# Centring the feed-forward tokens as two rounded products behind the fourth step's output product, with the square and the copy of the result in two places

## Chip, cores and metric

The kernel runs on one core of a Trainium2 chip. The metric is the device time of one execution, in microseconds (us).

## What is computed

The input is `x` of shape (4, 512, 128). First comes one mixing layer in closed form (a layer norm, an RWKV-style recurrence, a product), then a layer norm, and then six pairs of attention and feed-forward layers. The change lies in the layer norm of the feed-forward layer; cut to what matters:

```
for i in range(6):
    x = attn_layer(shift_tokens(x), ...) + x            # 16 heads of 64, windows of 32 tokens
    x = ffn_layer(shift_tokens(x), ...) + x

def shift_tokens(t):   # the second half of the channels comes from the token before
    a, s = split(t, 2, -1); s = pad(s, one token in front)[:, :-1]; return concatenate([a, s], -1)

def ffn_layer(x, g, bln, W1, b1, W2, b2):
    mu = x.mean(-1); var = ((x - mu) ** 2).mean(-1)
    xn = (x - mu) / sqrt(var + 1e-05) * g + bln
    a, gate = split(xn @ W1 + b1, 2, -1)
    return a * gelu(gate) @ W2 + b2
```

## The kernel before

**Tiles and items.** Channels lie on the 128 partitions, tokens along the free dimension. An item is one batch row (512 tokens) in one layer: 6 x 4 = 24 items. An item has four steps of 128 tokens, `t` = 0 to 3, so there are 96 steps, numbered through; ten more (`TAIL_STEPS`) drain the pipeline. In a step the attention of its tokens is begun (`project(step, ...)`), and work on earlier steps goes on: scores of step - 2, output product (`merge_heads`, L1497) of step - 3, transposes of the normed queries and keys of step - 1 and step - 2 (`turn_qk`, L1372).

**Order of the work.** Each engine has its own loop over the steps, and the order in it is written out by hand: POOL L891 to L952, DVE L1114 to L1149, ACT L1275 to L1312, TensorE (PE) L1594 to L1645. Between the engines there are only semaphores. Each engine executes strictly in its order, so that one wait holds up all that stands behind it. From step 12 to 95, waits that are implied by others are left out (`lean`, L1316).

**Two kinds of product.** Most products are made with `F32R` operands, a value split into a rounded part (`_hi`) and the rest (`_lo`): `project` (L1340 to L1342) is three passes of 512 columns, hi by hi, hi by lo, lo by hi. A plain float32 product, such as the centring, is one instruction in the kernel that the compiler makes into two (the trace counts them as x2).

**The feed-forward layer of item m** runs in the steps of the items behind it. In step t = 3 of item m + 1:
- `shift_tail` (ACT, L1223, copies L1227 and L1228, first thing in the step) writes the shifted tokens `xs2`.
- `centre` (PE, L1501, product L1509), behind the first two projections, multiplies `xs2` by `center` = I - 1/128 into `bank[5]`.
- `take_centred` (ACT, L1230), in front of `square(step, 0)`, squares the bank into `xsq` (L1236) and copies it to `xc` (L1237).
- `variance` (PE, L1511, products L1517), behind `turn_probs`, waits for both and multiplies `xsq` by a column of means into `bank[4]`. `project(step, V1)`, `turn_qk`, `weigh(step - 2, 0)` (L1465) and `turn_qk` stand behind it.
- `take_var` (DVE, L1082) moves four columns to `norm`.

At the start of step t = 0 of item m + 2 `root` (DVE, L1017 to L1025, nine small instructions, one root for the norms of queries and keys and for the variance) runs; `widen_rstd` (PE, L1526) spreads it over the partitions, `scale_xn` (DVE, L1090) multiplies `xc` by it, `bias_xn` (ACT, L1249, L1251) writes `xn_hi` and `xn`, `split_xn` (POOL, L875, L879) writes `xn_lo`, and `expand`, `gelu`, `gate` and `contract` follow. The score of step t = 0 waits for `scale_xn`.

**The other things that the steps below touch.** `rotate(step, c)` (DVE, L979 and L986) reads projection c for q0, q1, k0, k1; `square(step, c)` (ACT, L1188) squares the same bank behind it; `sum_squares` (DVE, L996) sums, POOL's `add` (L864) adds the rotated halves, and `normalise` (POOL, L872) multiplies by the root. `project(step, K1)` waits for `square(step, 1)` (L1336), since it writes the same bank. Steps with item%4 = 3 and t = 3 ("ending", 15, 31, 47, 63, 79) split two weights of the next layer on POOL (`split_weights`, L129 and L131); items with item%4 = 1 split the feed-forward weights at t = 2 and 3 (`split_w_1`, L908, L910), items with item%4 = 2 split two weights at the ends of t = 2 and t = 3.

**The mask of the scores** is written by `mask_cuts` (L1376) in one piece per product or in two or three; the cuts have no arithmetic meaning, each further piece is one more product. In step 6 `more` is 9.

## Time and profile before

| | |
|---|---|
| median of 3 runs | 1683.49 us (1682.31 to 1683.5) |
| the profiled execution | 1678.35 us |
| its span on the core | 1676.6 us |
| busy: PE / DVE / ACT / POOL | 94% / 86% / 66% / 64% |
| PE clock that was granted, mean over the span | 0.979 |

Read the engines' busy shares first, then the 40 slices, then the windows of single steps, and in a step the timeline of each engine with the idle time in front of an instruction and what ended it, in square brackets. PE is matmul, PEld its weight load, DVE VectorE, ACT ScalarE, POOL GpSimd. The ends of matmuls are modelled and overlap with the start of the next; so a matmul's cost is read from the distance between two starts.

### The profile page before, as it was taken

How to read it: one execution, taken by the hardware profiler on the slowest of the kernel's cores; microseconds unless marked ns; L12 is line 12 of the kernel's file. 1: busy time of each engine (PE TensorE's matmuls, PEld its weight loads, DVE VectorE, ACT ScalarE, POOL GpSimd, SP SyncE). 2: the span in 40 equal slices, each digit the busy share in tenths (PEclk: the TensorE clock that was granted, in tenths of full speed). 3: DMA queues.
4: the chain of work that ended last, by engine and by line, in shares of the span. 5: the costliest groups of instructions: out<-in, count | busy, mean ns of one | idle time of the engine just before them, and what ended most of it. 6: DMA issues, size and time to landing. Idle time of an engine off the chain costs nothing.

```text
span 1676.6 us, 77736 instructions
## 1 busy us (share of the span) xinstructions
PE 1568.2 (94%) x33168; PEld 1271.4 (76%) x33168; DVE 1447.6 (86%) x3173; ACT 1114.9 (66%) x2014; POOL 1068.4 (64%) x1040
## 2 busy tenths in 40 slices
PE   4469999999999999999999999999999999999987
PEld 2247888778878878888778788788887878887874
DVE  8969989889889888889989889888889888898862
ACT  4336677667677667677667766766776766776663
POOL 3646767676666666667576577585676575675640
PEclk7679999999999999999999999999999999999999
DMA  2011111211111211111211111211111111111110
GB/s 88 32 51 45 41 38 40 77 35 41 34 50 38 60 44 40 42 51 29 63 38 53 43 37 42 63 38 53 30 51 41 50 51 47 32 44 41 38 47 14
DMA packets 41086, 75.09 MB, mean 45 GB/s; under 512 B 9472, under 2 KB 22568, under 8 KB 40744
## 3 DMA queue, kind: packets, MB, share of 16 engines
q1 hardware_dynamic: 40744, 70.12, 14.4%
q8 instruction: 265, 4.34, 1.1%
q14 instruction: 77, 0.63, 0.1%
HBM read 20.08 MB, written 2.10 MB: 13 GB/s over the span
## 4 chain that ended last, share of the span: by engine, by line
PE 68%; issue 8%; POOL 8%; DVE 6%; ACT 5%; ACTq 0%; POOLq 0%; DVEq 0%
PE bank L1372 8%; PE bank L1340 7%; PE bank L1423 7%; PE bank L1497 7%; PE wide L1465 7%; PE bank L1342 6%; PE bank L1341 6%; PE bank L1482 4%; PE bank L1577 4%; PE bank L1442 3%; POOL qk L864 3%; POOL qk L872 2%; PE bank L1411 2%; PE bank L1549 2%; PE bank L1553 1%
## 5 line engine op out<-in xcount | busy, mean ns | idle before, releaser
L872 POOL TENSOR_TENSOR qk<-qk,rnorm 128x512 f32<-128x512 f32 x384 | 401.2, 1045 | 344.4 <-DVE rnorm L1025 344.4
L864 POOL TENSOR_TENSOR qk<-qk,qk_sin 128x512 f32<-128x512 f32 x384 | 491.8, 1281 | 146.3 <-DVE qk_sin L986 146.3
L1188 ACT ACTIVATE squares<-bank 128x512 f32<-128x512 f32 x384 | 229.5, 598 | 153.5 <-DVE qk_sin L986 153.3
L996 DVE TENSOR_REDUCE norm<-squares 128x8 f32<-128x512 f32 x384 | 258.5, 678 | 30.5 <-ACT squares L1188 28.3
L1340 PE MATMUL bank<-w_hi,xs_hi 128*128 128x512 f32 x576 | 263.5, 457 | 11.8 <-ACT squares L1188 6.6
L979 DVE TENSOR_TENSOR qk<-bank,tables 128x512 f32<-128x512 f32 x384 | 261.7, 682 | 8.8 <-PE bank L1342 8.6
L986 DVE TENSOR_TENSOR qk_sin<-bank,tables 128x512 f32<-128x512 f32 x384 | 261.4, 681 | 0.6 <-POOL qk L864 0.6
L1372 PE MATMUL bank<-ident,qk 128*128 128x128 f32 x1536 | 225.3, 278 | 6.1 <-POOL qk L872 5.3
L1342 PE MATMUL bank<-w_hi,xs_lo 128*128 128x512 f32 x576 | 228.9, 397 | 0.0
L1341 PE MATMUL bank<-w_lo,xs_hi 128*128 128x512 f32 x576 | 227.9, 396 | 0.4 <-issue 0.4
L1372 PEld LDWEIGHTS bank<-ident,qk 128*128 128x128 f32 x1536 | 180.8, 141 | 44.4 <-POOL qk L872 7.0
L1497 PE MATMUL bank<-o_t,w_o_s 128*128 128x128 f32 x1536 | 187.8, 276 | 2.5 <-DVE probs L1039 1.5
L1497 PEld LDWEIGHTS bank<-o_t,w_o_s 128*128 128x128 f32 x1536 | 179.1, 192 | 3.4 <-issue 3.1
L1465 PEld LDWEIGHTS wide<-v,p_t 64*32 64x32 f32 x12288 | 134.2, 105 | 61.5 <-issue 59.1
L1465 PE MATMUL wide<-v,p_t 64*32 64x65 f32 x12288 | 165.5, 225 | 1.8 <-DVE o L1052 1.1
L1031 DVE TENSOR_REDUCE row_max<-bank 128x8 f32<-128x512 f32 x192 | 123.7, 686 | 47.0 <-PE bank L1423 46.4
L1180 ACT COPY v<-bank 128x512 f32<-128x512 f32 x192 | 113.9, 593 | 75.6 <-PE bank L1342 74.8
L1423 PE MATMUL bank<-k_t,q_t 64*32 64x64 f32 x12288 | 150.4, 225 | 14.4 <-issue 14.1
L1219 ACT COPY o_t<-bank 128x512 f32<-128x512 f32 x192 | 112.3, 585 | 71.1 <-PE bank L1482 71.0
L1204 ACT ACTIVATE probs<-probs 128x512 f32<-128x512 f32 x192 | 121.0, 631 | 56.4 <-DVE probs L1039 50.7
L1423 PEld LDWEIGHTS bank<-k_t,q_t 64*32 64x32 f32 x12288 | 142.0, 105 | 21.5 <-issue 18.6
L1340 PEld LDWEIGHTS bank<-w_hi,xs_hi 128*128 128x128 f32 x576 | 109.7, 191 | 41.3 <-ACT squares L1188 14.3
(181 smaller groups left out, 2724.9 us busy)
## 6 DMA issues: line engine op xcount, KB each, us to landing
v<-v SPq DMA_DIRECT2D x96, 390.0 KB, 3.5
v<-v SPq DMA_DIRECT2D x72, 130.0 KB, 3.6
w_raw<-in_L_ffn_Wqkv SPq DMA_DIRECT2D x36, 256.0 KB, 3.2
w_o_s<-in_L_ffn_Wo SPq DMA_DIRECT2D x6, 512.0 KB, 3.9
w_raw<-in_L_ffn_W SPq DMA_DIRECT2D x6, 341.0 KB, 3.4
mix_x_nat<-in_L_attn_x SPq DMA_DIRECT2D x4, 256.0 KB, 3.4
w_raw<-x_res_scratch SPq DMA_DIRECT2D x4, 256.0 KB, 3.4
out<-w_raw SPq DMA_DIRECT2D x4, 256.0 KB, 3.2
```

The source lines that it names most:

```text
L864: pool.tensor_tensor(qk[:, g % 2, c, :], qk[:, g % 2, c, :], qk_sin[:, (QK_CHUNKS * g + c) % SINES, :], ALU.add).then_inc(added[c], 1)
L872: pool.tensor_tensor(view, view, rnorm[:, g % 2, c * HPC:(c + 1) * HPC].unsqueeze(2) .to_broadcast([P, HPC, DH]), ALU.mult).then_inc(norme ...
L979: dve.tensor_tensor(qk[:, g % 2, c, :].rearrange("p (h d) -> p h d", d=DH), src[:].rearrange("p (h d) -> p h d", d=DH), table(kind).unsque ...
L986: dve.tensor_tensor(qk_sin[:, (old + SINES) % SINES, :].rearrange("p (h a d) -> p h a d", a=2, d=DH // 2), src[:].rearrange("p (h a d) -> ...
L996: dve.tensor_reduce(norm2[:, c * HPC:(c + 1) * HPC], squares[:, c % 2, :].rearrange("p (h d) -> p h d", d=DH), AX.X, ALU.add).then_inc(sum ...
L1340: pe.matmul(bank_of(c)[:], l_hi, w_hi[:, n, :], start=True, stop=False)
L1341: pe.matmul(bank_of(c)[:], l_hi, w_lo[:, n, :], start=False, stop=False)
L1342: pe.matmul(bank_of(c)[:], l_lo, w_hi[:, n, :], start=False, stop=True).then_inc(projected[c], 1)
L1372: mm = pe.transpose(bank[2 + c % 2][:, j * P:(j + 1) * P], qk[:, g % 2, c, j * P:(j + 1) * P], ident[:])
L1423: mm = pe.matmul(bank[4 + r][WINDOW * h:WINDOW * (h + 1), col:col + 2 * WINDOW], q_t[row, pair, WINDOW * w:WINDOW * (w + 1)], k_t[row, pai ...
L1465: mm = pe.matmul(wide[WINDOW * h:WINDOW * (h + 1), w, quad * (DH + 1):(quad + 1) * (DH + 1)], p_t[row, r, 2 * s + m, WINDOW * h:WINDOW * ( ...
L1497: mm = pe.matmul(bank[4][:, 0:P], w_o_s[:, layer % 2, p, :], o_t[:, g % 2, p, :], start=(p == 0), stop=(p == PAIRS - 1))
```

## The change

`xs2` is split like the other F32R operands: ACT rounds it to `xs2_hi` (`round_tail`, in the place where `take_centred` was), POOL subtracts to `xs2_lo` (`split_tail`, between `normalise(step - 1, 0)` and the weight splits or `add(step, 0)`). The two share the memory of `xn_hi` and `xn_lo`. `centre` is two passes with the rounded `center_r`, and stands behind `merge_heads` in place of behind the projection of Q0. The square of the bank stands behind `square(step, 2)` on ACT, the copy `xc` is the first instruction of ACT in the next step (t = 0). `variance` waits for the square alone. Some waits of `score` and `merge_heads` are moved. In step 6 `mask_cuts` cuts six masks more (`more` 9 to 15). `center_r` is made once on DVE.

```diff
--- before.py
+++ after.py
@@ -664,7 +664,7 @@
     STEPS = BLOCKS + TAIL_STEPS
     PAD = WINDOW
     NORMS = QK_CHUNKS * HPC
-    N_CONST = 9
+    N_CONST = 10
     SINES = 3
     FIRST_SPLIT = 3 * NBLK
     with ExitStack() as ctx:
...
@@ -700,6 +701,8 @@
         w_1_hi, w_1_lo = sb("w_1_hi", [P, 2 * NHID, P], F32R), sb("w_1_lo", [P, 2 * NHID, P], F32R)
         xn_hi, xn_lo = sb("xn_hi", [P, SEQ], F32R), sb("xn_lo", [P, SEQ], F32R)
         x1, xs2, hidden = sb("x1", [P, 2, SEQ]), sb("xs2", [P, SEQ]), sb("hidden", [P, NHID, SEQ])
+        xs2_hi, xs2_lo = xn_hi, xn_lo
+        center_r = sb("center_r", [P, P], F32R)
         xc = xn = sb("xc_xn", [P, SEQ])
         xsq = gated = sb("xsq_gated", [P, SEQ])
 
...
@@ -876,14 +879,20 @@
                 if not real(m):
                     return
                 pool.wait_ge(xn_copied, 2 * (m + 1))
-                pool.tensor_tensor(xn_lo[:], xn[:], xn_hi[:].bitcast(F32), ALU.subtract).then_inc(xn_ready, 1)
+                pool.tensor_tensor(xn_lo[:], xn[:], xn_hi[:].bitcast(F32), ALU.subtract).then_inc(lo_ready, 1)
+
+            def split_tail(m):
+                if not real(m):
+                    return
+                pool.wait_ge(xs2_ready, 3 * (m + 1))
+                pool.tensor_tensor(xs2_lo[:], xs2[:], xs2_hi[:].bitcast(F32), ALU.subtract).then_inc(lo_ready, 1)
 
             def add_first_residual(m):
                 if not last(m):
                     return
                 b = m % BATCH
                 pool.wait_ge(x_res_loaded, 16 * (b + 1))
-                pool.wait_ge(xs2_ready, 2 * (m + 1))
+                pool.wait_ge(xs2_ready, 3 * (m + 1))
                 pool.tensor_tensor(x1[:, m % 2, :], x1[:, m % 2, :], x_res, ALU.add).then_inc(x1_full, 1)
 
             split_tokens(0, 0)
@@ -922,6 +931,8 @@
                 if opening:
                     split_weights(layer, K1)
                 normalise(step - 1, 0)
+                if t == 3:
+                    split_tail(item - 1)
                 if item % BATCH == 1 and item < ITEMS and t >= 2:
                     split_w_1(layer, t - 2)
                 if ending:
@@ -961,6 +972,7 @@
                 for j in (NHID - 1, 2 * NHID - 1):
                     dve.tensor_scalar(z[:, j, HID[-1]:P], ident[:, HID[-1]:P], 0.0, 0.0, ALU.mult, ALU.add).then_inc(constants_ready, 1)
             dve.memset(v[:, :, 1, :, DH:DH + 1], 1.0).then_inc(constants_ready, 1)
+            dve.tensor_scalar(center_r[:], center[:], 1.0, 0.0, ALU.mult, ALU.add).then_inc(constants_ready, 1)
             dve.wait_ge(constants_ready, N_CONST)
 
             def rotate(g, c):
@@ -1223,17 +1235,27 @@
                 if not real(m):
                     return
                 act.wait_ge(x1_done, NBLK * (m + 1))
-                need(act, centred, m)
+                need(act, lo_ready, 2 * m - 1)
                 act.copy(xs2[0:half, :], x1[0:half, m % 2, :]).then_inc(xs2_ready, 1)
                 act.copy(xs2[half:P, 1:SEQ], x1[half:P, m % 2, 0:SEQ - 1]).then_inc(xs2_ready, 1)
 
+            def round_tail(m):
+                if not real(m):
+                    return
+                act.wait_ge(xs2_ready, 3 * m + 2)
+                need(act, up_ready, NHID * m)
+                act.copy(xs2_hi[:], xs2[:]).then_inc(xs2_ready, 1)
+
+            def square_centred(m):
+                if not real(m):
+                    return
+                act.wait_ge(centred, m + 1)
+                need(act, hidden_ready, NHID * m)
+                act.activation(xsq[:], bank[5][:], ACT.Square).then_inc(cen_taken, 1)
+
             def take_centred(m):
                 if not real(m):
                     return
-                act.wait_ge(centred, m + 1)
-                need(act, hidden_ready, NHID * m)
-                need(act, up_ready, NHID * m)
-                act.activation(xsq[:], bank[5][:], ACT.Square).then_inc(cen_taken, 1)
                 act.copy(xc[:], bank[5][:]).then_inc(cen_taken, 1)
 
             def late_centred():
@@ -1280,6 +1302,8 @@
                     shift_tokens(item + 1, 0)
                 if t == 3:
                     shift_tail(item - 1)
+                if t == 0:
+                    take_centred(item - 2)
                 take_v(step, 0)
                 take_qk(step - 2, 0)
                 if t == 1:
@@ -1288,7 +1312,7 @@
                 if t == 0:
                     bias_xn(item - 2)
                 if t == 3:
-                    take_centred(item - 1)
+                    round_tail(item - 1)
                 square(step, 0)
                 take_o(step - 3, 0)
                 square(step, 1)
@@ -1301,6 +1325,8 @@
                 if t == 0 and item > 0:
                     shift_tokens(item, 1)
                 square(step, 2)
+                if t == 3:
+                    square_centred(item - 1)
                 take_probs(step - 2, 0)
                 take_probs(step - 2, 1)
                 if t == 2:
@@ -1376,7 +1402,7 @@
             def mask_cuts(step, product):
 
                 if step < FIRST_SPLIT:
-                    more = 9 if step == NBLK + 2 else 0
+                    more = 15 if step == NBLK + 2 else 0
                 else:
                     more = (9, 9, 0, 0)[step % NBLK]
                 if product + 2 * 4 < more:
@@ -1387,10 +1413,12 @@
                 if not live(g):
                     return
                 item, t = divmod(step, NBLK)
+                pe.wait_ge(qk_taken[1], g + 1)
                 if not lean(step, 3):
-                    for c in range(QK_CHUNKS):
+                    for c in (0, 2, 3):
                         pe.wait_ge(qk_taken[c], g + 1)
-                    need(pe, x1_done, g - 1)
+                    if not lean(step, 0):
+                        need(pe, x1_done, g - 1)
                     need(pe, shifted[0], g)
                     need(pe, shifted[1], g)
                 if t == 0:
@@ -1400,7 +1428,7 @@
                 if t == 2:
                     need(pe, x2_done, item - 1, ITEMS)
                 if t == 3:
-                    need(pe, cen_taken, 2 * item, 2 * ITEMS)
+                    need(pe, out_taken, item - 1 - (ITEMS - BATCH), BATCH)
                 if t == 0:
                     need(pe, var_taken, item - 1, ITEMS)
                 for h in range(4):
@@ -1490,6 +1518,7 @@
                 if not lean(g + 3, 2):
                     pe.wait_ge(w_o_loaded, 16 * (layer + 1))
                     pe.wait_ge(o_taken[0], g + 1)
+                if not (lean(g + 3, 2) or lean(g + 3, 3)):
                     pe.wait_ge(o_taken[1], g + 1)
                     need(pe, x1_done, g)
                 need(pe, shifted[0], g + 2, BLOCKS)
@@ -1501,17 +1530,18 @@
             def centre(m):
                 if not real(m):
                     return
-                pe.wait_ge(xs2_ready, 2 * (m + 1))
+                pe.wait_ge(lo_ready, 2 * m + 1)
+                need(pe, shifted[1], NBLK * (m + 1) + 2, BLOCKS)
                 if not lean(NBLK * (m + 1) + 3, 3):
-                    need(pe, shifted[1], NBLK * (m + 1) + 1, BLOCKS)
                     need(pe, x2_done, m, ITEMS)
                 need(pe, out_taken, m - (ITEMS - BATCH), BATCH)
-                pe.matmul(bank[5][:], center[:], xs2[:], start=True, stop=True).then_inc(centred, 1)
+                pe.matmul(bank[5][:], center_r[:], xs2_hi[:], start=True, stop=False)
+                pe.matmul(bank[5][:], center_r[:], xs2_lo[:], start=False, stop=True).then_inc(centred, 1)
 
             def variance(m):
                 if not real(m):
                     return
-                pe.wait_ge(cen_taken, 2 * (m + 1))
+                pe.wait_ge(cen_taken, 2 * m + 1)
                 need(pe, x1_done, NBLK * (m + 1) + 1, BLOCKS)
                 for j in range(NBLK):
                     mm = pe.matmul(bank[4][:, j:j + 1], xsq[:, j * P:(j + 1) * P], mean_col[:], start=True, stop=True)
@@ -1555,7 +1585,7 @@
                 if j == 0:
                     for dst, tile, signal in sides:
                         from_hi(dst, tile)
-                    pe.wait_ge(xn_ready, m + 1)
+                    pe.wait_ge(lo_ready, 2 * m + 2)
                     for dst, tile, signal in sides:
                         from_lo(dst, tile, signal)
                 else:
@@ -1598,10 +1628,6 @@
                 project(step, Q0)
                 if t == 1:
                     expand(item - 2, 2)
-                if step == BLOCKS + 3:
-                    keep_busy(5)
-                if t == 3:
-                    centre(item - 1)
                 if step == 0:
                     late_output()
                 weigh(step - 3, 1)
@@ -1623,6 +1649,10 @@
                     late_widen()
                 turn_qk(step - 1, 3, o_taken[1], step - 2)
                 merge_heads(step - 3)
+                if step == BLOCKS + 3:
+                    keep_busy(5)
+                if t == 3:
+                    centre(item - 1)
                 if t == 1:
                     contract(item - 2)
                 turn_probs(step - 2, 0)
```

## Rows read from the trace of the kernel before

**Rows 1.** Busy time by engine over the whole span, from the page.

```profile
PE 1568.2 (94%) x33168; PEld 1271.4 (76%) x33168; DVE 1447.6 (86%) x3173; ACT 1114.9 (66%) x2014; POOL 1068.4 (64%) x1040
PEclk7679999999999999999999999999999999999999
```

**Rows 2.** Windows, steps 35, 39, 43, 47, 48: length, then busy PE, PEld, DVE, ACT, POOL.

```profile
638.72:653.63 14.91, 14.91 (x343) 12.56 (x342) 13.61 (x32) 10.92 (x20) 9.72 (x9) 1.00 0.13 39
702.13:717.03 14.90, 14.90 (x344) 12.56 (x342) 13.61 (x32) 10.91 (x20) 11.39 (x13) 1.00 0.13 38
765.42:780.59 15.17, 15.17 (x344) 12.50 (x342) 14.61 (x32) 10.70 (x20) 12.15 (x13) 1.00 0.14 39
829.57:845.31 15.74, 14.97 (x343) 12.56 (x342) 14.45 (x33) 10.93 (x20) 13.09 (x13) 1.00 0.19 56
845.31:863.50 18.19, 16.86 (x359) 13.88 (x357) 14.96 (x33) 13.40 (x24) 15.01 (x15) 1.00 0.21 60
```

**Rows 3.** Timeline of PE, step 35: start, us, line, [idle before].

```profile
639.96 0.40 PE L1342 MATMUL bank<-w_hi,xs_lo 128*128 128x512 f32 x1
640.20 1.02 PE L1509 MATMUL bank<-xs,center 128*128 128x512 f32 x2
641.14 0.86 PE L1465 MATMUL wide<-v,p_t 64*32 64x65 f32 x64
...
647.21 1.95 PE L1497 MATMUL bank<-o_t,w_o_s 128*128 128x128 f32 x16
649.87 0.95 PE L1517 MATMUL bank<-mean_col,xsq_gated 128*128 128x1 f32 x8
```

**Rows 4.** Timeline of ACT and DVE in step 35.

```profile
641.25 0.61 ACT L1236 ACTIVATE xsq_gated<-bank 128x512 f32<-128x512 f32 x1
641.75 0.60 ACT L1237 COPY xc_xn<-bank 128x512 f32<-128x512 f32 x1
...
649.33 0.60 ACT L1188 ACTIVATE squares<-bank 128x512 f32<-128x512 f32 x1 [0.57 <-DVE qk_sin L986]
...
645.02 1.29 DVE L1031 TENSOR_REDUCE row_max<-bank 128x8 f32<-128x512 f32 x2 [0.67 <-PE bank L1423]
```

**Rows 5.** Groups by line and form.

```profile
L1169 ACT CAST xs_hi<-xs 128x256 fp32r<-128x256 f32 x48 | 19.5, 407 | 1.5
L1249 ACT ACTIVATE xn_hi<-xc_xn,vecs 128x512 fp32r<-128x512 f32 x24 | 17.3, 722 | 44.2 <-DVE xc_xn L1090 44.2
L879 POOL TENSOR_TENSOR xn_lo<-xc_xn,xn_hi 128x512 fp32r<-128x512 f32 x24 | 30.7, 1280 | 39.0 <-ACT xc_xn L1251 39.0
```

**Rows 6.** Timeline of POOL, DVE, PE around the end of step 47, then of step 43.

```profile
843.38 1.04 POOL L872 TENSOR_TENSOR qk<-qk,rnorm 128x512 f32<-128x512 f32 x1
844.38 1.27 POOL L864 TENSOR_TENSOR qk<-qk,qk_sin 128x512 f32<-128x512 f32 x1
...
844.61 1.07 DVE L1017 TENSOR_SCALAR norm<-norm 128x36 f32<-128x36 f32 x1
...
844.47 1.09 PE L1372 MATMUL bank<-ident,qk 128*128 128x128 f32 x8 [0.77 <-POOL qk L872]
...
780.33 1.29 POOL L131 TENSOR_TENSOR w_lo<-w_raw,w_hi 128x512 fp32r<-128x512 f32 x1
780.72 0.94 DVE L1017 TENSOR_SCALAR norm<-norm 128x36 f32<-128x36 f32 x1
```

**Rows 7.** Timeline around the centring of the last item (step 99).

```profile
1655.89 1.13 PE L1509 MATMUL bank<-xs,center 128*128 128x512 f32 x2 [0.75 <-ACT xs L1228]
...
1658.18 0.97 PEld L1517 LDWEIGHTS bank<-mean_col,xsq_gated 128*128 128x128 f32 x8 [0.79 <-ACT xc_xn L1237]
```

**Rows 8.** Instruction loads of PE: queue on the page; score of step 38.

```profile
q8 instruction: 265, 4.34, 1.1%
...
693.48 0.65 PE L1423 MATMUL bank<-k_t,q_t 64*32 64x64 f32 x39 [0.57 <-issue]
  issue: 32.7, 49
```

More of the change, by code:

```diff
@@ L685, in transformer @@
         squares = sb("squares", [P, 2, CHUNK])
-        norm2, root_t, root_w = (sb(name, [P, NORMS + NBLK]) for name in ("norm2", "root_t", "root_w"))
+        norms = sb("norms", [P, 3, NORMS + NBLK])
+        norm2, root_t, root_w = (norms[:, n, :] for n in range(3))
         rnorm = sb("rnorm", [P, 2, NORMS + NBLK])
@@ L727, in transformer @@
         xs_copied, xs2_ready, cen_taken = sem("xs_copied"), sem("xs2_ready"), sem("cen_taken")
-        xn_ready, gelu_done = sem("xn_ready"), sem("gelu_done")
+        lo_ready, gelu_done = sem("lo_ready"), sem("gelu_done")
         added, normed, xs_ready = sems("added", 4), sems("normed", 4), sem("xs_ready")
@@ L1225, in shift_tail @@
                 act.wait_ge(x1_done, NBLK * (m + 1))
-                need(act, centred, m)
+                need(act, lo_ready, 2 * m - 1)
                 act.copy(xs2[0:half, :], x1[0:half, m % 2, :]).then_inc(xs2_ready, 1)
                 act.copy(xs2[half:P, 1:SEQ], x1[half:P, m % 2, 0:SEQ - 1]).then_inc(xs2_ready, 1)
-            def take_centred(m):
+            def round_tail(m):
[5 more added lines that the diff above has]
+            def square_centred(m):
                 if not real(m):
@@ L1234, in take_centred @@
                 need(act, hidden_ready, NHID * m)
-                need(act, up_ready, NHID * m)
                 act.activation(xsq[:], bank[5][:], ACT.Square).then_inc(cen_taken, 1)
+            def take_centred(m):
+                if not real(m):
+                    return
                 act.copy(xc[:], bank[5][:]).then_inc(cen_taken, 1)
```

## The prediction

> **What bounds the kernel now.** The busy times come first: PE works 94% of the span, DVE 86%, ACT 66%, POOL 64% [rows 1]. The granted clock shows full speed (2.4 GHz) from the fourth slice to the end, and PE stays as busy as before in every step that is changed, so the clock is no term here. What matters is the stage that is changed, the steps t = 3. Their windows [rows 2] show four kinds. Step 35 (item%4 = 0) and 39 (item%4 = 1) last 14.91 and 14.90 us and PE is busy in all of it; step 43 (item%4 = 2) 15.17, again all of it; step 47 (an ending step) lasts 15.74 with PE idle for 0.77. DVE has 13.61 to 14.61 of work in the same windows, so it runs 0.6 to 1.3 us behind PE as the next bound, and POOL grows from 9.72 to 13.09. A PE that is never idle says that PE's own work bounds the step, but only as long as the saved time isn't larger than the room that the next engine leaves at the place where it is saved. That is the question of this change.
>
> A difference of 0.2% (3.4 us) is what a measurement of this kernel can tell from no change.
>
> **The saving on PE.** The plain float32 centring starts at 640.20 and the next product at 641.14 [rows 3]; in steps without it `weigh` stands 0.85 earlier, and the whole product is charged at 0.85. A rounded pass of 512 columns costs the distance of its neighbours, 639.96 to 640.20 = 0.24, mean 0.23. Two passes: 0.46. The saving is 0.39 per item, 24 x 0.39 = 9.4 us if it comes through. That is the upper end of the gain from this part; the lower end is zero or a loss, for what stands behind decides.
>
> **Where it comes through, step 35.** PE's front is 0.85 earlier, since the product leaves it. DVE can follow by 0.67 at most: that is its only idle time in front of `maximum`, ended by the score [rows 4]; from there it runs without a gap. The second half of the step is then paced by DVE's chain. `rotate(step, 2)` ends some 0.7 earlier, `square(step, 2)` starts at 9.85 after the step's start in place of 10.61 (649.33 less 638.72) [rows 4], ends at 10.45, and the square of the centred tokens stands behind it, ends about 0.5 later (two such instructions in a row are 0.50 apart, 641.25 and 641.75 [rows 4]), at 10.95. On PE the output product starts 0.82 earlier than 8.49 (647.21 less 638.72 [rows 3]), the new centring follows it, then `turn_probs`, and `variance` would be ready at 10.8. It waits for the square, which ends at 10.95, and its products start at 11.1. Before, they started at 11.15 (649.87 less 638.72 [rows 3]). `project(step, V1)`, `turn_qk` and `weigh` stand behind the waiting `variance`, and DVE's `normalise` and the root of the next step wait for `weigh`. So of 0.39 only 0.04 is left: 7 items of this kind (item%4 = 0, and the first and last), 7 x -0.04 = **-0.3 us**.
>
> **The square and the copy.** Moving the square is the step above. The copy `xc` (0.60 each [rows 4]) goes into the first microsecond of t = 0, where ACT idles for 1.0 to 1.5 us; `scale_xn` needs it 3 us later. Cost nothing; without that cover it would be 0.5. The cast `round_tail` has no row of its form; half of it takes 0.407, the biased one of full size 0.722 [rows 5]: between 0.6 and 0.72, in a slot that lost 1.2. Nothing, and ACT is earlier rather than later.
>
> **POOL's split.** `split_tail` has the form of L879, 1.280 us [rows 5], and every instruction of POOL behind it in t = 3 moves by 1.28 less POOL's idle time in front of `add(step, 3)`. In step 35 that idle time is 1.72: free. In step 39, where `split_w_1` takes 1.8 of the same step (POOL 11.39 [rows 2]), `add(step, 3)` ends 0.3 later than DVE wants to start the root. DVE's L1017 takes 0.17 alone; where a POOL instruction of two operands runs, it ends when that ends: 1.07 beside L864 (844.38, 1.27), 0.94 beside L131 (780.33, 1.29) [rows 6]. So 0.10 per item, 5 items: **+0.5 us**. In step 43 DVE has no gap at all (14.61 of 15.17 [rows 2]), K1 waits for DVE's chain whatever PE's front does, and the new 0.46 behind `merge_heads` is added in full: V1 comes 0.8 later, of which the stall that t = 0 has in any case (1.33 in step 48 [rows 2]) takes most; L131, at the end of POOL's queue, ends 0.26 later and holds the root. 5 x 0.26 = **+1.3 us**.
>
> **The ending steps** carry the largest term. In step 47 POOL runs without a gap to 845.65, and PE already waits 0.77 for its L872 (843.38 to 844.42) [rows 6]. 1.28 more in front of it delays `turn_qk` by 1.28 and the nine root instructions of DVE get caught between POOL's later instructions: L872 and L864 now lie where the root wants to run. PE's delay alone would be taken up by the 1.33 of idle time in step 48 [rows 2]; the root's would not, because the chain root, widen, scale, score is what makes that idle time. Lower bound 0 (DVE gets through between two POOL instructions each time), upper bound 1.28; I take 1.0, near the upper end, since L1017 in the step before was held to the end of L864. 5 x 1.0 = **+5.0 us**.
>
> Here a rule of the Trainium skill bears on it. What the rows show is L1017 held to the end of the POOL instruction. The page "SBUF — State Buffer", section "Who interferes with whom", says that VectorE and GpSimd share one pair of ports as an exclusive lock, taken for a whole instruction by whoever issues first, and the trace agrees (1.07 and 0.94 against 0.17).
>
> **The tail.** In step 99 the chain is bare: the copies, centring at 1655.89, square, copy, variance at 1658.18, for which PE waited 0.79 [rows 7]. Added: cast 0.65, split 1.28 with two handovers of some 0.1; taken off: the copy from `variance`'s wait 0.5, the passes 0.4, and idle overlaps. **+1.0 us**.
>
> **Instruction loads.** PE's instructions come in 265 loads [rows 8], 16 KB each by 4.34 MB/265, and 32.7 us in 49 cases the score waited for "issue" and for nothing else; in 21 of them it is the score at t = 2, as in step 38 (0.57 [rows 8]), mean 0.8. An item has the same count of PE instructions before and after, so the place of the loads in the item is fixed and is shifted by the six extra mask pieces of step 6, which are 12 instructions (with the two moved ones 10). Bounds: the stall goes (21 x 0.8 = -17) or grows by as much (+17) or stays; I take zero, as a shift by 10 in a score of 256 instructions and 1.46 us moves the boundary by 0.06 us. The Trainium skill, "Runtime: NRT & Kernel Launch", section "Instruction fetch mechanics", has loads of 256 instructions that are "mostly hidden"; the trace disagrees here, with 0.57 us open in step 38. By that sentence the shift would be worth nothing.
>
> **Sum.** -0.3 + 0.5 + 1.3 + 5.0 + 1.0 = +7.5 us on the profiled execution's 1678.35, giving 1685.9. The median of the runs shown is 1683.49, 5.1 above that execution, so the forecast is 1683.5 + 7.5 = 1691.0.
>
> **Rivals.**
> - *The stall of the score at t = 2 gets shorter* by half: the load is asked for a little earlier, when slow products instead of short ones are in front. 21 x -0.4 = -8.4; with the sum above -0.9: 1682.6. For it: the stall is short of its end by a fraction of a microsecond. Against: no row shows what sets the request.
> - *The stall goes entirely*, -16.8, net -9.3: 1674. The faster side. It decides from a load that is asked for 0.8 us earlier, at one place, the score at t = 2.
> - *The centring's saving comes through*: `variance` isn't held by the square, since DVE's chain moves with PE's front, and the ending steps' delay disappears in step 48. 24 x -0.39 plus the tail's 1.0 is -8.4: 1675. For it: PE is busy 14.91 of 14.91 [rows 2]. Against: the order on ACT, square behind `square(step, 2)`.
> - *DVE's root gets through in the ending steps*: the 5.0 falls away, +2.5, 1686. Against: in step 47 the first of the nine was held already [rows 6].
> - *A load falls into a bare place* in each item: 24 x 0.5 = +12 above the sum, 1703.
> That the change doesn't do what it says has little room: the two passes have the form of L1340's.
>
> **How the numbers follow.** Main case 0.40 (its own range 1687.5 to 1695); stall halved 0.18; stall gone 0.20; saving through 0.14; root gets through 0.04; worse 0.04. Faster by over 0.2%: 0.20 + 0.14 = 0.34. Same: 0.18 + 0.04 = 0.22. Slower: 0.44. The range reaches from the faster cases at 1672 to the upper end of the main case, 1695 (the ending steps at their bound of 1.28 and a little of the plain steps), and leaves out the worse case and the far end of the faster ones.
>
> **What the profile after would show.** Right: two products 0.23 apart behind L1497; `variance` with an idle time in front that ACT's square ends; steps 35 and 39 within 0.1 of 14.9; ending steps and openings together 1 us longer, with L1018 or L1019 of DVE at about 1 us; step 43 longer by 0.3; the tail 1 us later. Wrong: t = 3 steps of 14.5 us; or t = 2 steps below 13.8 with no `issue` in L1423, which would make it faster by loads alone.

## The result and the profile after

The change makes the kernel slower: 1689.12 us median (1688.82 to 1690.08, 5 runs) against 1682.31 (1681.62 to 1683.5, 5 runs), a ratio of 1.0038, 95% interval 1.0026 to 1.005. Run again on two other chips it was 1.0052 (1.0038 to 1.0065) and 1.0067 (1.0052 to 1.0082). The forecast was 1691.0, and 7.5 us of loss for 6.8 measured here; by the two other ratios it is 8.7 and 11.3.

The two profiled executions lie further apart than the medians: spans of 1688.3 and 1676.6. So a difference between these two traces has to be split into what comes in every execution and what doesn't, before it is given to the change. Lines are shifted in the new kernel: L1340 is L1366, L1372 is L1398, L864 is L867, L872 is L875, L1017 to L1025 are L1029 to L1037, L1236 is L1254, the centring is L1538 and L1539, POOL's new split L888, `variance` L1547.

From the page of the changed kernel, busy time by engine:

```profile
PE 1570.7 (93%) x33173; PEld 1273.8 (75%) x33174; DVE 1449.5 (86%) x3174; ACT 1124.2 (67%) x2038; POOL 1098.2 (65%) x1064
```

Against [rows 1] POOL has 29.8 us more, that is 24 x 1.24, and PE, which was to get 9 us less, has 2.5 more; part of that is the low clock below, at which the same products count as busy for longer. The windows of the same steps, 35, 39, 43, 47 and 48, with their length first and then PE, PEld, DVE, ACT, POOL:

```profile
640.34:655.19 14.85, 14.80 (x343) 12.52 (x342) 13.52 (x32) 11.23 (x21) 10.95 (x10) 1.00 0.13 38
703.50:718.48 14.98, 14.94 (x344) 12.46 (x341) 13.65 (x32) 11.26 (x21) 12.33 (x14) 1.00 0.13 38
766.84:782.77 15.93, 15.21 (x343) 12.48 (x342) 14.60 (x32) 11.22 (x21) 13.85 (x14) 1.00 0.13 37
831.33:848.51 17.18, 15.08 (x343) 12.76 (x342) 15.78 (x35) 11.25 (x21) 14.54 (x14) 0.99 0.26 74
848.51:866.77 18.26, 18.01 (x357) 14.77 (x356) 14.29 (x30) 13.36 (x24) 14.79 (x15) 0.92 0.08 22
```

They answer to [rows 2]: 14.91 has become 14.85, 14.90 is 14.98, 15.17 is 15.93, 15.74 is 17.18. In the ending step PE idles 2.10 us where it idled 0.77. The last column but two is new as well: the granted clock is below 1 in steps 47 and 48.

The second half of step 35 (it starts at 640.34), timeline of PE and then of ACT:

```profile
649.70 0.48 PE L1538 MATMUL bank<-xn_hi,center_r 128*128 128x512 f32 x1
650.02 0.39 PE L1539 MATMUL bank<-xn_lo,center_r 128*128 128x512 f32 x1
650.25 1.04 PE L1470 MATMUL bank<-ident,probs 128*128 128x128 f32 x8
651.34 1.05 PE L1547 MATMUL bank<-mean_col,xsq_gated 128*128 128x1 f32 x8
651.33 0.97 PEld L1547 LDWEIGHTS bank<-mean_col,xsq_gated 128*128 128x128 f32 x8 [0.29 <-ACT xsq_gated L1254]
...
650.20 0.60 ACT L1200 ACTIVATE squares<-bank 128x512 f32<-128x512 f32 x1 [0.56 <-DVE qk_sin L998]
650.69 0.59 ACT L1254 ACTIVATE xsq_gated<-bank 128x512 f32<-128x512 f32 x1
```

The second pass starts 0.32 after the first and the next product 0.55 after it, where the plain product took 0.94 to the next one [rows 3]: 0.39 less, so the cheap product is there. The squares start at 9.86 and 10.35 after the step's start and the second ends at 10.94; `variance` starts at 11.00, where it started at 11.15 [rows 3]. The weight load of `variance` waited 0.29 for that square, as the bracket in its row says: this is the wait that was forecast.

The end of step 47, POOL, DVE and PE, against [rows 6]:

```profile
845.67 0.72 POOL L860 TENSOR_TENSOR xs_lo<-xs,xs_hi 128x256 fp32r<-128x256 f32 x1
846.31 0.17 DVE L1029 TENSOR_SCALAR norms<-norms 128x36 f32<-128x36 f32 x1
846.36 1.03 POOL L875 TENSOR_TENSOR qk<-qk,rnorm 128x512 f32<-128x512 f32 x1
846.52 0.92 DVE L1030 TENSOR_SCALAR rnorm<-norms 128x36 int32<-128x36 int32 x1
847.36 1.26 POOL L867 TENSOR_TENSOR qk<-qk,qk_sin 128x512 f32<-128x512 f32 x1
847.44 1.42 PE L1398 MATMUL bank<-ident,qk 128*128 128x128 f32 x8 [2.05 <-POOL qk L875]
847.47 1.21 DVE L1031 TENSOR_TENSOR norms<-norms,rnorm 128x36 f32<-128x36 f32 x1
848.71 0.20 DVE L1032 TENSOR_TENSOR norms<-norms,rnorm 128x36 f32<-128x36 f32 x1
```

Two of the nine root instructions are held, the second (0.92) until POOL's L875 ends (847.39), the third (1.21) until its L867 ends (848.62); free, they take 0.2. PE waits 2.05 for L875.

**All steps by kind.** A step's length is the distance from its first `project` product to that of the next step. Means of the steps from item 3 to 22 (five of each kind; of the third four, without step 91, whose length differs from profile to profile: 15.6 before, 16.3 changed, 20.9 in E3), in us; the columns behind are the experiments below:

| step | before | changed | E1 | E2 | E3 | E6 | E7 | E9 | E10 |
|---|---|---|---|---|---|---|---|---|---|
| t=3, item%4=0 | 14.91 | 14.85 | 14.85 | 14.49 | 15.01 | 14.65 | 15.82 | 14.64 | 14.32 |
| t=3, item%4=1 | 14.90 | 14.96 | 14.84 | 14.51 | 15.07 | 14.98 | 15.82 | 14.96 | 14.34 |
| t=3, item%4=2 | 15.16 | 15.95 | 15.94 | 15.17 | 16.09 | 15.73 | 16.92 | 15.94 | 15.18 |
| t=3, ending | 15.75 | 17.08 | 15.90 | 15.75 | 15.75 | 17.60 | 16.73 | 15.90 | 15.75 |
| t=0, item%4=0 (behind an ending step) | 18.18 | 17.94 | 18.18 | 17.97 | 18.18 | 18.01 | 18.18 | 18.17 | 17.96 |
| t=0, item%4=1 | 17.12 | 17.11 | 17.10 | 17.11 | 17.11 | 16.96 | 17.11 | 16.95 | 17.47 |
| t=0, item%4=2 | 17.11 | 17.18 | 17.11 | 17.11 | 17.12 | 17.17 | 17.11 | 17.18 | 17.55 |
| t=0, item%4=3 | 17.95 | 17.33 | 17.11 | 17.96 | 17.11 | 17.59 | 17.12 | 17.35 | 17.89 |

Each row t = 0 stands behind one t = 3: the stall in it can take up what the step in front has lost. Changed less before: ending 1.33 - 0.24 = 1.09, item%4 = 2 0.79 - 0.62 = 0.17, item%4 = 1 0.06 + 0.07 = 0.13, item%4 = 0 -0.06 - 0.01 = -0.07. Times five: 5.4 + 0.8 + 0.7 - 0.3 = 6.6 us. Outside these kinds, the steps t = 2 of the same items are 1.5 us shorter in sum and those with t = 1 unchanged within 0.2.

**The clock.** In the changed kernel the clock falls to half (1.2 GHz) four times after the start: in steps 47 and 79, both times right when PE goes on after the 2 us of idling in an ending step, and twice in the tail. In the profile of before it never does. Windows of 3.4 us behind the end of step 47, of 3 us in the tail of the changed kernel, and one in the tail of before at the same work:

```profile
848.30:851.71 3.41, 3.41 (x42) 2.37 (x41) 1.75 (x8) 1.53 (x3) 1.89 (x3) 0.53 0.48 131
1647.52:1650.52 3.00, 3.00 (x17) 3.00 (x16) 0.00 (x0) 1.10 (x2) 0.00 (x0) 0.55 0.00 0
1659.52:1662.52 3.00, 2.17 (x10) 1.82 (x9) 0.00 (x0) 0.58 (x1) 0.00 (x0) 0.50 0.00 0
```

```profile
1641.19:1644.19 3.00, 3.00 (x15) 1.80 (x14) 0.29 (x1) 0.47 (x1) 0.00 (x0) 1.00 0.00 0
```

An ending step and the step behind it last 35.45 and 35.46 us together where the clock fell, 34.71 to 34.74 in the three other pairs, and 33.92 to 33.97 before. So a fall costs 0.7 us, and of the 5.4 us of the ending steps about 4.0 (5 x 0.79) are the wait and 1.4 the clock. It comes with PE's wait of 2 us: in the six profiles with the split in this place of POOL's queue (changed, E4, E5, E6, E11, E12) PE idles 2.04 to 2.19 us there and the clock fell at the end of 20 of 30 ending steps. In before, E1, E2, E3, E7, E8, E9 and E10 it idles 0.5 to 1.4 us and the clock fell at none of 40. In the tail the output products of 16 take 3.52 and 3.51 us where before they take 2.02, and from the first of them to the centring it is 21.45 us for 15.81; 2.0 of these 5.6 are the wait below, so that about 3.7 us of the 5.4 that the tail is longer are clock. The low clock there doesn't need the change: E2 and E10, which keep the old order, have it in their tails too. The rest is the change's, in the chain of the last item:

```profile
1666.48 0.62 ACT L1247 CAST xn_hi<-xs 128x512 fp32r<-128x512 f32 x1
1667.18 1.26 POOL L888 TENSOR_TENSOR xn_lo<-xs,xn_hi 128x512 fp32r<-128x512 f32 x1 [34.90 <-ACT xn_hi L1247]
1668.49 0.50 PE L1538 MATMUL bank<-xn_hi,center_r 128*128 128x512 f32 x1 [2.73 <-POOL xn_lo L888]
1669.94 1.02 PE L1547 MATMUL bank<-mean_col,xsq_gated 128*128 128x1 f32 x8
```

PE waits 2.73 for the split where it waited 0.75 [rows 7], 2.0 more; centring to `variance` is 1.45 for 2.29, 0.8 less: +1.1 us, rounded from the two starts. So of the 11.7 us between the two profiles 6.6 are the steps', 1.1 the tail's and 3.7 the tail's clock, and about 0.3 is left over. That remainder is a balance: step 0 starts 1.1 us later in the changed kernel, which wasn't followed, and the steps t = 2 are 1.5 us shorter.

### The profile page after: what moved, and what is told of

Its sections match the earlier page's. It is cut to its first block, busy times and chain, and to the rows that moved or that the text cites. A ratio compares the mean times of both kernels' runs of the same rounds, so it can differ in the third digit from the quotient of the medians.

```text
span 1688.3 us, 77817 instructions
## 1 busy us (share of the span) xinstructions
PE 1570.7 (93%) x33173; PEld 1273.8 (75%) x33174; DVE 1449.5 (86%) x3174; ACT 1124.2 (67%) x2038; POOL 1098.2 (65%) x1064
## 4 chain that ended last, share of the span: by engine, by line
PE 54%; DVE 15%; issue 12%; POOL 8%; ACT 6%; ACTq 0%; DVEq 0%; POOLq 0%
PE bank L1451 6%; PE bank L1398 6%; PE wide L1493 6%; PE bank L1366 6%; PE bank L1368 5%; PE bank L1367 5%; PE bank L1526 4%; PE bank L1607 4%; PE bank L1510 3%; POOL qk L867 3%; DVE norms L1008 3%; DVE qk_sin L998 3%; DVE qk L991 2%; DVE probs L1051 2%; POOL qk L875 2%
## 5 line engine op out<-in xcount | busy, mean ns | idle before, releaser
L875 POOL TENSOR_TENSOR qk<-qk,rnorm 128x512 f32<-128x512 f32 x384 | 401.0, 1044 | 340.7 <-DVE rnorm L1037 340.7
L867 POOL TENSOR_TENSOR qk<-qk,qk_sin 128x512 f32<-128x512 f32 x384 | 491.7, 1280 | 128.3 <-DVE qk_sin L998 128.3
L1008 DVE TENSOR_REDUCE norms<-squares 128x8 f32<-128x512 f32 x384 | 255.9, 676 | 30.3 <-ACT squares L1200 28.2
L1366 PE MATMUL bank<-w_hi,xs_hi 128*128 128x512 f32 x576 | 264.6, 459 | 14.6 <-ACT squares L1200 9.4
L1398 PE MATMUL bank<-ident,qk 128*128 128x128 f32 x1536 | 224.7, 277 | 12.6 <-POOL qk L875 11.2
L1398 PEld LDWEIGHTS bank<-ident,qk 128*128 128x128 f32 x1536 | 179.7, 141 | 51.3 <-POOL qk L875 13.5
L1451 PE MATMUL bank<-k_t,q_t 64*32 64x64 f32 x12288 | 150.7, 225 | 15.4 <-issue 15.3
L1366 PEld LDWEIGHTS bank<-w_hi,xs_hi 128*128 128x128 f32 x576 | 109.5, 190 | 46.9 <-ACT squares L1200 19.4
```

The costliest lines, as they stand in the source:

```text
L867: pool.tensor_tensor(qk[:, g % 2, c, :], qk[:, g % 2, c, :], qk_sin[:, (QK_CHUNKS * g + c) % SINES, :], ALU.add).then_inc(added[c], 1)
L875: pool.tensor_tensor(view, view, rnorm[:, g % 2, c * HPC:(c + 1) * HPC].unsqueeze(2) .to_broadcast([P, HPC, DH]), ALU.mult).then_inc(norme ...
L1008: dve.tensor_reduce(norm2[:, c * HPC:(c + 1) * HPC], squares[:, c % 2, :].rearrange("p (h d) -> p h d", d=DH), AX.X, ALU.add).then_inc(sum ...
L1366: pe.matmul(bank_of(c)[:], l_hi, w_hi[:, n, :], start=True, stop=False)
L1398: mm = pe.transpose(bank[2 + c % 2][:, j * P:(j + 1) * P], qk[:, g % 2, c, j * P:(j + 1) * P], ident[:])
L1451: mm = pe.matmul(bank[4 + r][WINDOW * h:WINDOW * (h + 1), col:col + 2 * WINDOW], q_t[row, pair, WINDOW * w:WINDOW * (w + 1)], k_t[row, pai ...
```

## The experiments

Every time is compared with the kernel before on the same chip (median there 1679.4 us for E1 to E4, 1681.3 for E5 to E12).

**E1: POOL's split cut to four columns** (changed kernel; the low parts of the other columns are left out of the centring).

```
- pool.tensor_tensor(xs2_lo[:], xs2[:], xs2_hi[:]..., ALU.subtract)
+ n = SEQ if m == 0 else 4
+ pool.tensor_tensor(xs2_lo[:, 0:n], xs2[:, 0:n], xs2_hi[:, 0:n]..., ALU.subtract)
```

> The changed kernel, with POOL's split of the tokens cut to 4 columns (for every item but the first), so that POOL's added 1.28 us goes and all handovers stay; the low parts of the other columns are left out of the centring. Theory (POOL's instruction is what costs, above all in the ending steps): the ending steps fall from 17.0 to 17.2 us to about 16.0 and the steps behind them stay at 17.7 to 18.2, the steps with item%4 = 1 lose 0.1, the end of the kernel 1.2; in all 6 to 7 us less than the changed kernel, about 1682.5. Rival (the place of the centring and ACT's order cost, not POOL): at most 1.5 us less, about 1688.

1682.08 us, ratio 1.0013 (0.9997 to 1.003). The theory holds: the ending steps are at 15.90 with 18.18 behind them. On the same chip the changed kernel with nine mask cuts (E4) is 10.1 us slower than this. Windows of steps 47 and 48:

```profile
829.50:845.40 15.90, 14.90 (x344) 12.45 (x341) 14.57 (x33) 11.24 (x21) 13.27 (x14) 1.00 0.20 58
845.40:863.57 18.17, 16.88 (x359) 13.87 (x357) 14.96 (x33) 13.45 (x24) 15.00 (x15) 1.00 0.21 56
```

POOL has 1.27 us less than in the changed kernel's 14.54 and PE's idle time is 1.00. Also item%4 = 2 loses nothing now: 15.94 in front, but 17.11 for 17.33 behind.

**E2: two rounded passes in the old place** (kernel before, operands that are there anyway, so another product; rounding and split left out).

```
- pe.matmul(bank[5][:], center[:], xs2[:], start=True, stop=True)
+ pe.matmul(bank[5][:], stand_in, xs_hi[:], start=True, stop=False)
+ pe.matmul(bank[5][:], stand_in, xs_hi[:], start=False, stop=True)
```

> The kernel before, with the plain product replaced in its old place by two rounded passes of 512 columns over operands that are there anyway (so it computes another product; the splitting of xs2 is left out). It shows what the cheaper product alone is worth. Theory (the saving is there in the steps where PE is never idle and is eaten by the new order): steps t = 3 with item%4 = 0 and 1 fall from 14.90 to about 14.5, the others stay at 15.16 and 15.75; 12 x 0.39 = 4.7 us, about 1677.5. Rival (DVE is the next bound at once): these steps stay above 14.8 and the time within 1.5 us of the kernel before. Second rival (it comes through everywhere): 9.4 us, 1673.

1675.65 us, ratio 0.9976 (0.9961 to 0.9991), 4 us less. The steps with item%4 = 0 and 1 are at 14.49 and 14.51, the others don't move, and 18.18 falls to 17.97: ten steps of 0.4 plus 5 x 0.2. So the saving of the cheaper product exists, in half of the steps. Window of step 35:

```profile
636.00:650.49 14.49, 14.49 (x343) 12.54 (x342) 13.61 (x32) 10.93 (x20) 9.75 (x9) 1.00 0.13 39
```

**E3: the plain product in the new place** (changed kernel without rounding and split; `center` by `xs2`, one product).

> The changed kernel with the plain float32 product in the new place and without the rounding and the split; it computes what the reference has. Theory: POOL's cost goes (ending steps down by 1, end of the kernel down by 1.9), and the product's 0.39 comes on top in the steps with item%4 = 0, 1 and 2, which rise to about 15.2, 15.3 and 16.3; in all within 2 us of the changed kernel, about 1688. Rival (POOL's split is harmless): 24 x 0.39 = 9.4 above the changed kernel, about 1698.

1686.01 us, ratio 1.0039 (1.0021 to 1.0057). The pattern is the theory's: ending steps back at 15.75 and 18.18, the others up by 0.11 to 0.16 over the changed kernel. The size isn't: the plain product costs these steps at most 0.16 more than two passes, not 0.39; that the wait for the square hides the rest is argued, not shown. Nor does the table account for the time: by it E3 would be 1.8 us above the kernel before, and the ratio says 6.6. In the profiled execution 5.3 us more come from one step, 91, of 20.92 us for 15.6: PE idles 2.88 us for `issue`, and the clock is at half for 6.8 us from 0.8 before the end of that gap. Whether the other executions have it isn't known. So E3 by itself leaves open what the new place costs; E1 and E9, which have the same place, are at ratios of 1.0013 and 1.0005.

**E4 and E12: nine mask cuts in step 6**, the second time beside the changed kernel (E11).

> The changed kernel with the mask cuts of step 6 back at 9, that is 12 instructions of PE fewer. Theory (the shift of the instruction loads is worth nothing): within 1.5 us of the changed kernel, steps t = 2 between 13.7 and 14.9 as before. Rival (the six cuts move the loads to a better place, and this hides a larger loss): 8 us slower, about 1697, with longer gaps by issue in the score, or in other steps than t = 2.

> The changed kernel with 9 mask cuts again, now beside it on one chip. The first look had 12 us above the kernel before, against 7 to 8 for the changed kernel on other chips, with the same idle time by issue in the score. Theory (the six cuts are worth nothing): within 1.5 us of the changed kernel. Rival (they are worth some): 3 to 5 us above it.

E4 1692.17 us, ratio 1.0074 (1.005 to 1.0098), which left it open; E12 1690.35, ratio 1.0051 (1.0036 to 1.0067), beside 1692.92 for E11. The six cuts gain nothing that shows here. The line `issue: 32.7, 49` of [rows 8] adds the idle times of PE and of its weight load, so that most stalls count twice; the matmuls alone idle 14.1 us in 23 cases before, 15.3 in 25 in the changed kernel, 15.2 in 25 in E4 and 15.7 in 24 in E12. What the cuts do shows in the place of the gap. Timeline of PE in step 38, changed and E4:

```profile
694.81 0.69 PE L1451 MATMUL bank<-k_t,q_t 64*32 64x64 f32 x44 [0.37 <-issue]
696.38 0.64 PE L1451 MATMUL bank<-k_t,q_t 64*32 64x64 f32 x38 [0.43 <-issue]
```

Before, 39 products stood behind the gap [rows 8]. So the changed kernel has it five products earlier, which with their weight loads are the 10 instructions forecast, and E4 one product later than before.

**E5 and E11: the changed kernel again.**

> The changed kernel once more, on the chip of the next three, as their measure. Expected 6 to 8 us above the kernel before (the first comparison gave 6.8). It tells also whether the slower clock near the end that its first profile shows comes in each execution: theory, it comes by chance (the profiles of the experiments so far have it in part), and its about 4 us explain why the two first profiles were 11.7 apart and the medians 6.8.

> The changed kernel beside the next one: 6 to 9 us above the kernel before.

1689.24 us (ratio 1.0052) and 1692.92 (1.0067). E5's tail has one stretch at half clock, E11's two, as in the first profile. Of the other profiles, one each, E4, E9, E10 and E12 have two or three, E1, E2, E6 and E7 one, before, E3 and E8 none (the last 3 us of a profile left out). The mean granted clock of the timed executions is 0.975 to 0.982 for the kernel before and 0.972 to 0.978 for the changed one: in the tail the low clock seems to come in both, and in the changed one the ending steps' is added.

**E6: variance later** (changed kernel).

```
  turn_probs(step - 2, 1)
- if t == 3: variance(item - 1)
  project(step, V1)
  turn_qk(step - 1, 2, ...)
  weigh(step - 2, 0)
+ if t == 3: variance(item - 1)
```

> The changed kernel with variance on PE moved behind V1, turn_qk and weigh, and take_var on DVE to the end of the step. Theory (in the steps with item%4 = 0 and 1 the saving of 0.39 is held by variance, which waits for the late square with V1 and weigh behind it): these steps fall from 14.85 and 14.97 to about 14.5 and 14.65, item%4 = 2 from 15.94 by 0.3, 4 to 6 us less than the changed kernel in all. Rival (DVE bounds these steps, whatever PE's order): they stay within 0.1, and the time within 1 us.

1691.44 us, ratio 1.0059 (1.0041 to 1.0078): no gain in all, and both halves of the answer stand in the table. Item%4 = 0 falls to 14.65 and the step behind it to 16.96, together 0.35 under the changed kernel and 0.42 under the kernel before, the whole saving of the product. Item%4 = 1, where POOL's last instruction holds the root, stays. The ending steps get worse, 17.60 for 17.08: with `weigh` and the root 0.7 earlier, three root instructions instead of two are held by POOL's (0.62, 0.98 and 1.19 us in step 63), and the clock fell in all five (in step 63 for 6.8 us in place of 3.4).

**E7: the split first on POOL** (changed kernel; `round_tail` behind `shift_tail`, `split_tail` in front of `normalise(step - 1, 3)`).

> The changed kernel with the rounding on ACT right behind the two copies and POOL's split first in the step, in the 2.5 us in which POOL waits for the root. Theory (the cost is POOL's instruction in front of a queue without a gap): of its 1.28 some 0.6 still lies outside the wait, so the ending steps fall by about 0.7 each, the steps with item%4 = 1 by 0.1; 3 to 4 us less than the changed kernel. Rival (ACT's copy of v, 0.65 later, holds the projection Q1): all steps t = 3 get 0.3 longer, and it gains nothing.

1699.85 us, ratio 1.012 (1.0102 to 1.0138), 10 us worse than the changed kernel, by neither of the two. Timeline of POOL and DVE at the start of step 35:

```profile
644.36 1.31 POOL L888 TENSOR_TENSOR xn_lo<-xs,xn_hi 128x512 fp32r<-128x512 f32 x1 [2.11 <-ACT xn_hi L1247]
644.56 1.16 DVE L1036 SCALAR_TENSOR_TENSOR norms<-norms,rnorm 128x32 f32<-128x32 f32 x1
645.75 0.19 DVE L1037 SCALAR_TENSOR_TENSOR rnorm<-norms,rnorm 128x32 f32<-128x32 f32 x1
```

The idle time that the split was put into is the root's: POOL waits there because DVE works out the root, and a split beside it holds the root's eighth instruction for 1.16 in place of 0.19. The plain steps t = 3 get 0.9 to 1.0 longer than in the changed kernel. An ending step is 0.35 shorter than there, but with the step behind it still 1.0 longer than before (34.91 for 33.94).

**E8: variance later in the kernel before**, the same edit.

> The kernel before with the same move of variance and take_var as in the run before last. Theory: there variance waits for nothing, PE is busy in all of the step and the same work in another order gains nothing in t = 3; weigh and the root come up to 0.3 earlier, which may take 0.1 to 0.3 from the stall at the start of t = 0: 0 to 5 us less than the kernel before. Rival (the place is worth as much here as there): 6 us or more.

1682.52 us, ratio 1.0014 (1.0003 to 1.0026), a little slower: the steps with item%4 = 0 and 1 are 0.2 longer (15.12 for 14.91 and 14.90); those with item%4 = 2 are 0.3 longer, and the step behind them is 0.3 shorter. So the place is worth something only where `variance` waits. What the 0.2 is wasn't followed.

**E9: mixed.** Plain product where the centring falls into an ending step and for the last item, two passes elsewhere, variance later in the steps with item%4 = 0.

> The changed kernel with the plain product (in the new place, with 4 columns left of the rounding and the split) for the items whose centring falls into an ending step and for the last one, and with variance and take_var later in the steps with item%4 = 0 alone. It computes all that the reference does. Theory (the cost is POOL's split in the ending steps; variance's wait holds the saving where POOL has room): ending steps 15.8 with 18.2 behind them, item%4 = 0 at 14.65 and 0.16 less in the step behind, the end of the kernel 1 us shorter than in the changed kernel; 5.4 + 2 + 1 = 8 us less than the changed kernel, that is level with the kernel before or up to 2 us under it. Rival (the ending steps' cost is the place of the centring): at most 3 us less than the changed kernel.

1682.31 us, ratio 1.0005 (0.9994 to 1.0016): level with the kernel before, and 10.6 us under the changed kernel on the same chip (E11), for 8 expected. Windows of steps 35, 47 and 48:

```profile
640.00:654.65 14.65, 14.65 (x343) 12.44 (x342) 14.06 (x34) 11.16 (x21) 10.95 (x10) 1.00 0.14 41
831.14:847.03 15.89, 15.14 (x343) 12.45 (x342) 14.34 (x33) 10.91 (x21) 13.25 (x14) 1.00 0.18 54
847.03:865.19 18.16, 16.86 (x358) 13.88 (x357) 14.96 (x33) 13.40 (x24) 14.98 (x15) 1.00 0.22 60
```

That is the theory's pattern. No version here beats the kernel before and computes all that it does.

**E10: one pass in the old place** (kernel before; ACT's two copies write the tokens rounded, their low part is left out).

> The kernel before in its old order, with the shifted tokens written rounded by the same two copies of ACT and one rounded pass in place of the plain product: neither POOL nor ACT gets work, and the low part of the tokens is left out (also the rounding of one tile of the last item's gelu is new). Theory: PE's charge falls from 0.85 to 0.23; in the steps with item%4 = 0 and 1 DVE has 0.67 us in front of the maximum, so nearly all of it comes through, 14.3 us in place of 14.9, nothing in the others; 6 to 8 us under the kernel before, 2 to 3 under the kernel with two passes in the old place. Rival (DVE bounds these steps at 14.5): as that one, 4.5 us under.

1684.54 us, ratio 1.0018 (1.0006 to 1.0031), slower. The steps t = 3 did what the theory said, 14.32 and 14.34. But over items 3 to 22 the steps t = 1 got 6.3 us longer in sum, t = 2 3.3, and t = 0 behind item%4 = 0 and 1 4.0, for 5.7 saved in t = 3 with item%4 = 0 and 1. From start to start the score products of these items take 11.8 us more than before. PE's idle time by `issue` in the score of the whole kernel is 25.5 us in 39 cases, for 14.1 in 23. Timeline of PE in steps 45, then 49:

```profile
806.74 0.89 PE L1427 MATMUL bank<-k_t,q_t 64*32 64x64 f32 x68 [0.47 <-issue]
...
872.53 0.88 PE L1427 MATMUL bank<-k_t,q_t 64*32 64x64 f32 x67 [0.73 <-issue]
```

One item later the gap stands one product later in the score: 68 products are left behind it, then 67, and 66 and 65 in steps 53 and 57. The centring as one pass is two instructions of PE shorter, a product and a weight load: the trace has 2816 records of PE per item in the kernels before and changed, and 2814 in E10. So the load boundaries no longer fall on the same place in each item; they wander through it and meet bare places. (The Trainium skill, "Runtime: NRT & Kernel Launch", section "Instruction fetch mechanics", has loads of 256 instructions each, fetched ahead. By that 11 loads are 2816 instructions, and an item two shorter shifts the boundary by two: the trace agrees, 68, 67, 66, 65 with a weight load to each product. The Trainium skill calls the crossing of a boundary "mostly hidden" there, and by number the trace agrees: of the 265 loads before, 23 show an idle time of PE in the score.)

## Why the prediction was right, and where not

- **The saving on PE**, 0.39 where it comes through: right. E2 has 0.40. The passes are 0.23 apart there and 0.32 in the changed kernel, where the next product follows 0.23 behind them; the pair costs 0.39 less than the plain product in both.
- **Step 35, eaten by the late square**: right, -0.04 forecast and -0.07 measured, `variance` at 11.00 for 11.1. The weight load of `variance` waits 0.29 for the square, and E6 shows the cause: with `variance` out of the way, 0.35 comes back.
- **POOL's split in front of `add(step, 3)`** (item%4 = 1): 0.10 forecast, 0.13 measured; gone in E1.
- **Item%4 = 2**: V1 0.8 later and most of it taken by the stall behind, right (0.79 and 0.62); 0.17 left for 0.26, 0.9 us for 1.3 in the sum. E1 says by what: without the split nothing is left. (The prediction's "DVE has no gap at all" in step 43 is not exact; it has one of 0.22.)
- **The ending steps**: 1.0 each forecast, 1.09 measured, but only 0.79 of it is the wait; 0.3 is the clock, which the forecast had at nothing. 0.15 is left without the split (E1) and none with the plain product (E3). The place in the root was right too; that it would be held twice, at its second and third instruction, the step had only as its upper end.
- **The tail**: 1.0 forecast, 1.1 measured for the chain.
- **The instruction loads**: zero forecast, and nothing that shows in the times (E12). The shift by 10 instructions is in the trace. But the stall was priced too high: "21 x 0.8" was read from the line that adds PE and its weight load. PE alone idles 11.9 us in 20 cases at t = 2, 0.6 each, so that the bound of 17 and the two rivals on the loads were too large by 1.4. E10 shows that the term is large once the number of instructions per item changes. To set one load with 0.57 us open against the "mostly hidden" of the Trainium skill, "Runtime: NRT & Kernel Launch", section "Instruction fetch mechanics", was a wrong reading too: 23 of 265 show in the score.
- **The clock** is the term that was missed. "PE stays as busy as before in every step that is changed, so the clock is no term here" overlooked the forecast's own 1.3 us more of waiting in the ending steps. It cost 0.7 in two of five ending steps of the first profile. A fall stands beside an `issue` gap of 2.0 to 2.9 us in step 91 of E3 and E9 and in step 7 of E10 as well, but E6 has gaps of 2.1 and 2.9 us without one: the length of the idle stretch alone doesn't decide. In the tail it accounts for about 3.7 us of that profile, and what brings it there stays open: PE idles 1.5 us in front of the output product in all the profiles, with a fall and without. E2 and E10, in the old order, have it, so the kernel before seems to have it in some of its executions.

The sum, -0.3 + 0.7 + 0.8 + 5.4 + 1.1 = 7.7 us, is 0.2 above the one forecast. That it comes so close is partly luck: the wait in the ending steps was 1.0 smaller than forecast and item%4 = 2 0.5 smaller, and 1.4 of clock that wasn't in the sum makes up for it. The forecast also gave its main case only 0.40 and "slower" 0.44, and its range, 1672 to 1695, takes in the faster rivals too; that the time lies in it says little. The terms are what the runs bear out. Of the rivals on the faster side, the one by which the saving comes through in full fell with the order on ACT, as the text against it said; the two by which the stall of the loads goes, or is halved, fell with the profile after, where PE's idle time by `issue` in the score is no less (15.3 us for 14.1; at t = 2 11.5 for 11.9).

## What to carry to other kernels

A cheaper product on the engine that bounds a step gains only if what stands behind it in the same queue doesn't wait for the helper of another engine, and if the engine that prepares its operands has room in the step where it has least. Look at the fullest kind of step, not at the mean: five ending steps of 96 carried 5.4 of 7.7 us, 1.4 of it through the clock. Idle time of POOL is no free place as long as DVE works in it on what POOL waits for.

## What the runs showed that was not expected

- PE idling 2.04 to 2.19 us in an ending step was followed by 3.4 us at half clock (once 6.8) in 20 of 30 cases, at 0.7 us each in the first profile; idling of 0.5 to 1.4 us there in none of 40.
- POOL's instruction with two operands in SBUF held DVE's small root instructions to its end: 0.92 and 1.21 us for 0.2 (changed kernel), 1.16 for 0.19 (E7). The Trainium skill, "SBUF — State Buffer", section "Who interferes with whom", has the two share ports with an exclusive lock; the trace agrees. With POOL's queue without a gap, two of the nine root instructions are held one behind the other, three in E6.
- Two instructions of PE fewer per item cost more than their product saved: 11.8 us more in the score products of items 3 to 22 and PE's idle time by `issue` in the score at 25.5 for 14.1, against 7.0 saved in the steps t = 3 of these items; the ratio was 1.0018 where 0.996 was expected.
